# Attention block with adapter: down projection on 128 weight columns, and the last two chunks' feed-forward ends rearranged

## The reference

```python
# adapter, one expert of 16 per sequence
hidden = gelu(x @ down_W.T + down_b)                 # 256 -> 64
hidden = hidden @ Wsel.T + bsel + domain_emb[idx]
x = layernorm(hidden @ up_W.T + up_b + x) * gamma + beta
# block, 16 heads of 16 features
scale, shift = split(silu(sin_emb(timestep)) @ W_ada + b_ada)
x = ln(x) * (1 + scale) + shift
scores = where(mask, -inf, q @ k.T / 4 + attention_bias)     # 512 x 512 per head
x = x + softmax(scores) @ v @ Wo + bo
h = ln(x) * g2 + beta2
x = x + gelu2(h @ W1 + b1) @ W2 + b2                 # 256 -> 1024 -> 256
```

## Time and profile before

| | |
|---|---|
| median of 3 runs | 948.84 us (948.53 to 948.96) |
| profiled execution, whole time | 954.04 us |
| profiled execution, span of its instructions | 952.3 us |
| busy: PE, PE weight loads, DVE, ACT, POOL | 893.7, 663.0, 703.0, 704.5, 705.4 us |
| mean granted TensorE clock | 0.984 |
| moved by DMA | 207.4 MB |

### The profile page before, as it was taken

The page is one execution under the profiler, slowest core; times in us unless marked ns, Lnnn a source line. Parts: engine busy times, 40 slices in busy tenths (PEclk is TensorE's granted clock), DMA queues, the critical chain, the costliest instruction groups (busy, mean ns, idle before and its releaser), DMA issues. The chain is left out here.

```text
span 952.3 us, 20729 instructions
## 1 busy us (share of the span) xinstructions
PE 893.7 (94%) x6476; PEld 663.0 (70%) x6476; DVE 703.0 (74%) x1904; ACT 704.5 (74%) x1670; POOL 705.4 (74%) x411
## 2 busy tenths in 40 slices
PE   5858889999999999999999999999999999999987
PEld 2535555777777776777777776777777777677766
DVE  5647778878687886878687886888787887675651
ACT  2347869878697787878797887878687787867641
POOL 2736997888777976988787986879787987784700
PEclk9789999999999999999999999999999999999998
DMA  6489969766997779776897769776897669765300
GB/s 191 141 250 315 320 192 284 225 217 205 269 274 209 221 207 289 218 228 205 261 275 216 225 209 287 219 228 209 240 271 219 203 200 287 231 184 163 99 12 12
DMA packets 147951, 207.41 MB, mean 218 GB/s; under 512 B 14393, under 2 KB 62330, under 8 KB 147842
## 3 DMA queue, kind: packets, MB, share of 16 engines
q1 hardware_dynamic: 145458, 204.10, 71.9%
q10 hardware_dynamic: 2384, 1.97, 0.8%
HBM read 185.03 MB, written 20.99 MB: 216 GB/s over the span
## 5 line engine op out<-in xcount | busy, mean ns | idle before, releaser
L509 POOL TENSOR_TENSOR bias_s<-mask_f,bias_s 128x1024 f32<-128x1024 f32 x256 | 601.3, 2370 | 138.0 <-DMA bias_s<-in_bias 137.5
L1505 DVE CUSTOM_DVE_ANT_0 bias_s<-sc,bias_s 128x512 f32<-128x512 f32 x512 | 347.8, 684 | 172.4 <-PE sc L879 160.7
L1085 ACT ACTIVATE bias_s<-bias_s,mx 128x512 f32<-128x512 f32 x512 | 371.2, 725 | 84.1 <-DVE mx L1505 81.9
L886 PE MATMUL tp<-ident,bias_s 128*128 128x128 f32 x2048 | 309.6, 274 | 6.2 <-ACT pT L1091 2.7
L886 PEld LDWEIGHTS tp<-ident,bias_s 128*128 128x128 f32 x2048 | 250.9, 141 | 88.0 <-ACT bias_s L1085 14.0
L1091 ACT COPY pT<-tp 128x512 f32<-128x512 f32 x335 | 195.0, 582 | 99.3 <-PE tp L886 96.7
L879 PE MATMUL sc<-stk,stq 128*128 128x512 bf16 x512 | 195.8, 383 | 22.1 <-DVE mx L1505 16.3
L808 PE MATMUL la<-w_s,act_s 128*128 128x256 f32 x512 | 128.2, 380 | 0.2 <-DVE act_s L1462 0.2
L1512 DVE COPY pT<-tp 128x512 f32<-128x512 f32 x177 | 121.1, 684 | 3.7 <-PE tp L886 3.6
L844 PE MATMUL pv<-pT,v_all 128*32 128x256 f32 x2048 | 123.8, 382 | 0.0
L793 PE MATMUL lc<-hT,w_s 128*128 128x256 f32 x464 | 121.2, 385 | 2.5 <-ACT hT L1040 1.9
(11 more groups left out here) (204 smaller groups left out, 812.9 us busy)
## 6 DMA issues: line engine op xcount, KB each, us to landing
bias_s<-in_bias SPq DMA_DIRECT2D x256, 512.0 KB, 4.6
stk<-k_parts SPq DMA_DIRECT2D x128, 96.0 KB, 3.8
stq<-q_parts SPq DMA_DIRECT2D x126, 96.0 KB, 4.0
k_parts<-kb SPq DMA_DIRECT2D x32, 192.0 KB, 2.3
q_parts<-qb SPq DMA_DIRECT2D x30, 192.0 KB, 2.4
xT<-in_x_t SPq DMA_DIRECT2D x8, 512.0 KB, 7.1
k_parts<-kb SPq DMA_DIRECT2D x32, 128.0 KB, 2.3
stk<-k_parts SPq DMA_DIRECT2D x64, 64.0 KB, 4.0
```

Source lines behind the costliest of these rows:

```text
L509: pool.tensor_tensor(tile, mask_f[:, :, :], tile, ALU.subtract).then_inc(s["masked"], 1)
L886: last = pe.transpose(tp[n % 2][:, kt * P:(kt + 1) * P], bias_s[:, n // 2 % NB, n % 2, kt * P:(kt + 1) * P], ident[:, :])
L1085: act.activation(tile, tile, ACT.Exp, bias=mx[:, t:t + 1], scale=-1.0, accum_out=sums[:, j, head_of(hh):head_of(hh) + 1]).then_inc(s["prob ...
L1505: dve.tensor_tensor_reduce(out=tile, in0=sc[t % 2][:, :], in1=tile, scale=1.0, scalar=BIG, op0=ALU.add, op1=ALU.min, accum_out=mx[:, t:t + ...
```

## The change

Four things change. `down_w` becomes 128 columns wide, POOL sets its columns 64 to 127 to zero as its first instruction, and the down matmul writes all 128 partitions of `lc`. PE waits for this clear before the first down matmul. `turn_rows` is booked at 13.0 in place of 12.6. The w2 quarters of chunk 14 are spread: the first four at 26.6, 27.6, 28.6 and 30.3, and the last four in iteration 16 at 10.3, 10.6, 11.0 and 11.3, between `wo` and `ht`; its `out` and `store` follow at 12.3 and 13.0. In chunk 15 the rows 128 to 255 of w2 go to bank `pv`, and both `out` and `store` are done in two halves, the first once four quarters of w2 are through.

```diff
-PE_AT = dict(up=0.3, v=(1.0, 2.0), q=(8.6, 10.0), xt1=12.6, k=(15.6, 16.3), down=(24.3, 25.3),
+PE_AT = dict(up=0.3, v=(1.0, 2.0), q=(8.6, 10.0), xt1=13.0, k=(15.6, 16.3), down=(24.3, 25.3),
...
     if f == NCH - 2:
...
-                  gate=(22.3, 23.3, 26.3, 28.0), w2=(26.6, 27.0, 28.0, 29.0, 29.3, 29.6, 30.3, 31.3), out=32.3,
-                  store=33.0)
+                  gate=(22.3, 23.3, 26.3, 28.0), w2=(26.6, 27.6, 28.6, 30.3, 42.3, 42.6, 43.0, 43.3), out=44.3,
+                  store=45.0)
     if f == NCH - 1:
...
-                  gate=(15.0, 15.6, 16.3, 17.0), w2=(17.3, 17.6, 18.0, 18.3, 18.6, 19.0, 19.3, 19.6), out=20.0,
-                  store=21.0)
+                  gate=(15.0, 15.6, 16.3, 17.0), w2=(17.3, 17.6, 18.0, 18.3, 18.6, 19.0, 19.3, 19.6), half=18.6, out=20.0,
+                  store_half=20.0, store=21.0)
...
-        down_w = sb("down_w", [P, CT, A])
+        down_w = sb("down_w", [P, CT, P])
...
+        def w2_rows(f, j):
+            return pv[:, 0:D] if f == NCH - 1 and j == 1 else la[:, j * D:(j + 1) * D]
...
-            load("down_in", [(down_w[:, :, :], downT.rearrange("(c p) a -> p c a", p=P))])
+            load("down_in", [(down_w[:, :, 0:A], downT.rearrange("(c p) a -> p c a", p=P))])
...
-                        if at == ffn_at(f)["store"]:
+                        when = ffn_at(f)
+                        if f == NCH - 1 and at in (when["store_half"], when["store"]):
+                            j = 0 if at == when["store_half"] else 1
+                            if j == 0:
+                                sp.wait_ge(s["d_out_half"], 1)
+                            else:
+                                sp.wait_ge(s["d_out"], f + 1)
+                            sp.dma_start(out_v[f][:, j, :], outb[:, j * D:(j + 1) * D]
+                                         ).then_inc(s["out_half_out"] if j == 0 else s["out_out"], 16)
+                        elif at == when["store"]:
...
+            link(pool.memset(down_w[:, :, A:P], 0.0))
             link(pool.memset(powc[:, :], -0.5))
...
-                last = pe.matmul(lc[0:A, :], down_w[:, ct, :], xT[:, ct, :], start=(ct == 0), stop=(ct == CT - 1))
+                last = pe.matmul(lc[:, :], down_w[:, ct, :], xT[:, ct, :], start=(ct == 0), stop=(ct == CT - 1))
...
             pe.wait_ge(s["down_in"], 16)
+            pe.wait_ge(s["pool_chain"], 1)
...
-                        rows = la[:, j * D:(j + 1) * D]
+                        rows = w2_rows(f, j)
...
+                        if k == 3 and f == NCH - 1:
+                            last.then_inc(s["p_w2_half"], 1)
...
-                    if at == when["out"]:
+                    if f == NCH - 1 and at in (when["half"], when["out"]):
+                        j = 0 if at == when["half"] else 1
+                        if j == 0:
+                            dve.wait_ge(s["p_w2_half"], 1)
+                            dve.wait_ge(s["g_x2"], f + 1)
+                            dve.wait_ge(s["out_out"], 16 * f)
+                        else:
+                            dve.wait_ge(s["p_w2"], f + 1)
+                        cols = slice(j * D, (j + 1) * D)
+                        dve.scalar_tensor_tensor(out=outb[:, cols], in0=w2_rows(f, j), scalar=0.5,
+                                                 in1=x2s[f % 2][:, cols], op0=ALU.mult, op1=ALU.add
+                                                 ).then_inc(s["d_out" if j else "d_out_half"], 1)
+                    elif at == when["out"]:
```

More of the change, by code:

```diff
@@ L314, in build @@
             d_recip a_wide p_rin a_rin d_ctx p_wo d_x2 a_x2 d_mv2 g_rs2 d_hn p_ht a_hT g_x2 p_w1 a_th d_act
-            p_w2 d_out out_out eff_parts emb0_ready emb0_sum half_p half_hi half_rest half_mid half_lo""".split()
+            p_w2 d_out p_w2_half d_out_half out_half_out out_out eff_parts emb0_ready emb0_sum half_p half_hi half_rest half_mid half_lo""".split()
         s = {n: sem(n) for n in names}
@@ L486, in _ @@
             each_iteration(body)
+            sp.wait_ge(s["out_half_out"], 16)
             sp.wait_ge(s["out_out"], 16 * NCH)
@@ L1327, in values @@
                 if c == 0:
-                    dve.wait_ge(s["pool_chain"], 3)
+                    dve.wait_ge(s["pool_chain"], 4)
                 dst = v_all[b % 2][:, 2 * (c % 2):2 * (c % 2) + 2, HD:].rearrange("p j (h e) -> p j h e", e=2 * HD)
```

## The result

| | before | changed |
|---|---|---|
| median | 948.68 us (948.20 to 948.96, 4 runs) | 938.69 us (938.12 to 939.65, 4 runs) |
| profiled execution, span | 952.3 us | 936.5 us |
| mean granted clock | 0.984 | 0.985 |

The ratio is 0.9888, interval 0.987 to 0.9906; by the medians that is 10.0 us faster. The forecast was 940.1, with a range from 938.7: the direction and the mechanisms were right, the gain was forecast 1.3 us too small, and the median lies 0.01 us under the range. Two terms of the sum were too small, the down projection (2.44 for 2.95 us) and the end (0.20 for about 0.7 us).

A forecast was written before the change was run, and what follows sets the result against it. PE was taken to bound the kernel from 147 to 800 us, with the last 39 us read from the timeline. 2.44 + 3.2 + 2.86 + 0.20 = 8.7 us off 948.84 gave 940.1 us, range 938.7 to 943.2.

The forecast's parts named there:

- the down projection: PE's down calls on 128 columns: ten in iterations 3 to 11 save 0.24 us each, 2.44 us; iteration 1 nothing.
- the end: Last rows: DVE's half out takes 0.48 in place of 0.68 us, saving 0.20; the half store's landing gives nothing.
- slots: Last slots of iteration 15: fewer w2 quarters on PE bring the spread 3.2 us earlier, ends 2.5 and 3.45.
- clock: Iteration 16: PE's clock stays at 1.00 with the pause filled, saving 2.86 us, with 0 as other end.
- The bounds of iteration 1, of the slots and of the stores: Uncertainties of those three places, said to put the main forecast by itself at 939.0 to 941.3 us.
- How the numbers follow: Step giving the main forecast chance 0.70, faster 0.96, the 8-in-10 range, and 0.2%, 1.9 us, as distinguishable from no change.
- The longer weight loads: Down calls: 54 ns more for each of 24 loads, hidden under the matmul before, so nothing; exposed 1.3 us.
- Rows at 13.0: Booking turn_rows at 13.0 leaves PE's instruction order and waits as they were: cost exactly 0.
- Quarters in iteration 16: Four moved w2 quarters, 3.45 us, fit between wo and ht with 0.96 us to spare and cost nothing.
- Rivals A to D: A clock falls, 943.0, 0.11; B down-call gains nothing, 942.6, 0.07; C ACT or DVE sets slots, 942.3, 0.08; D slower, 0.02.

The follow-up runs named there:

- w65: The changed kernel with 65 weight columns in the down projection in place of 128: 940.13 us, ratio 0.9905.
- down128_only: The kernel before with only the down projection on 128 weight columns and its clear: 945.07 us, ratio 0.9962.
- start_fill: The changed kernel with 2 and 5 unread products put into two PE waits of the start-up: 940.43 us, ratio 0.9893.
- best: The changed kernel with 2 and 5 unread products in two start-up waits and turn_rows booked at 13.3: 936.66 us, ratio 0.9852.

## Why the prediction was off, point by point

- The sum was near: by the stages behind the start-up, the change is worth 2.95 (down projection) + 3.20 (slots) + about 0.7 (halves) + 1.5 to 2.8 (clock), together about 8.3 to 9.6 us. I had 8.7.
- **The step that failed** is the size of two terms of the sum, with the bounds that were built on them. "Down projection" counted two places where a call loses time and put the transposes behind it at nothing: 2.44 us where 2.95 was measured. "The end" put the landing of the half store at nothing: 0.20 where about 0.7 was measured. With these two the same sum is 9.7 us and gives 939.1. The bounds of iteration 1, of the slots and of the stores covered neither.
- **The lower end of the range was too near as well**, at the step "How the numbers follow". It took three runs, 0.4 us apart, as the spread of this kernel. All runs of the kernel before lie within 946.9 to 953.1 us, those of the changed kernel within 938.1 to 942.4; between profiles up to 6 us lie in the start-up and 1.3 us in the price of the clock's fall. That the profiled execution stood 5.2 us above the median was the sign, and I carried it over as a constant in place of asking where it lay. The 0.4 us from 939.1 to the measured 938.69 is less than this spread and has no cause of its own on record.
- That the median fell 0.01 us outside and not inside is chance: of the ten runs of the changed kernel, eight lie in the range and two in the 0.6 us below it, and the median of all ten is 939.4.
- Down projection: mechanism right in that the width decides (`w65` puts the step between 64 and 65 columns), no gain in iteration 1 right, the term mis-sized: 2.95 and not 2.44, since the transposes behind the call lost 0.05 us each time too, and I read only the starts on either side of it. The longer weight loads cost nothing, as said.
- Rows at 13.0: 0, right.
- Slots: 3.2 forecast, 3.20 measured in every profile that has the moved quarters.
- Quarters in iteration 16: `wo` to `ht` 6.13 us as before, cover of 0.68 us left where I had 0.96; right.
- Clock: kept, right. The 2.86 us was the price in the one profile that I had; in `down128_only` the same fall costs 1.5 us.
- The end: 0.20 forecast, about 0.7 measured. DVE's half took 0.425 us, not 0.48, and the half store landed 0.5 us sooner. I had taken the landing of a 128 KB store of keys (2.3 us) as the nearest row; it was no guide to a store of output.
- Rivals A to D did not come.

## What to carry to other kernels

A group of float32 matmuls on 64 weight columns between groups on 128 is worth padding when PE sets the pace: count what its neighbours lose too, not only the group. Work that has to be done anyway does double duty in a pause of PE that would cost the clock, and a long pause can even be worth filling with products that nobody reads. And before a range is given from three runs that agree, look in the profile for stretches where the clock may fall or not: their whole price belongs in it.

## What the runs showed of the hardware that I had not expected

- 65 weight columns cost as little as 128, and 64 cost 0.295 us a call (two records of 512 columns) more: 0.09 in front, 0.15 behind, 0.05 in the transposes after.
- Two executions of one program differ by 4 us, most of it because the clock of a 12 us stretch of the start-up was 1.00 in one and 0.59 in the other, while the 797 us behind it agree to 0.04 us.
- The fall from 2.4 to 1.2 GHz after the same pause of 4.1 us cost 1.5 us in one profile and 2.8 in another.
- The products of `start_fill` and `best` kept the clock at 1.00 from 46 to 52 us in both, but the fall from 28 to 40 us came in one of them and not in the other.
- Stores of 128 KB of output landed after 1.7 us, those of 256 KB after 2.2; stores of 128 KB of keys in the kernel before took 2.3.
